# Splitting fp32 weights on GpSimd: gate/up part and down part with signals of their own

## The reference

```
x = x + tanh(g_xattn[0]) * attention(layernorm(x), ctx)          # 154 keys
x = x + tanh(g_ffn[0])   * sum over 8 experts e of
          (silu(xn @ Wg[e]) * (xn @ Wu[e])) @ Wd[e]              # 256 -> 1024 -> 256
x = x + tanh(g_xattn[1]) * multi_head_attention(layernorm(x), ctx)
x = x + tanh(g_ffn[1])   * top-1 mixture of 8 experts, 256 slots each
```

## Time and profile before

| | us |
|---|---|
| median of 3 runs | 1388.63 |
| lowest, highest | 1377.47, 1392.26 |
| the profiled execution | 1381.46 |
| its span, first to last instruction | 1379.6 |

### The profile page before, as it was taken

One profiled execution on the slowest core, in us unless ns is written; L12 is line 12 of the kernel. 1 busy time (PEld: TensorE's weight loads), 2 busy tenths in 40 slices (PEclk: granted clock), 3 DMA queues, 4 the chain that ended last, 5 costly groups with the idle time before them and its releaser, 6 DMA issues.

```text
span 1379.6 us, 18833 instructions
## 1 busy us (share of the span) xinstructions
PE 1268.5 (92%) x6162; PEld 1011.2 (73%) x6162; DVE 910.8 (66%) x1654; ACT 627.9 (46%) x1320; POOL 499.5 (36%) x501
## 2 busy tenths in 40 slices
PE   6979999999999999999999999999999999989945
PEld 4758777777777777777777777777777757767744
DVE  4886676666666666677666666666667647667533
ACT  2444444454444454444444445445444434443510
POOL 2342443333333344444333333344444003233324
PEclk9979999999999999999999999999999999999968
DMA  4040000100000000000100000000000321011033
GB/s 125 24 146 0 24 23 32 38 24 24 24 24 24 24 24 24 23 24 24 40 30 24 24 23 24 23 24 24 23 24 1 107 80 34 32 65 47 19 119 119
DMA packets 46646, 54.42 MB, mean 39 GB/s; under 512 B 4445, under 2 KB 42386, under 8 KB 46431
## 3 DMA queue, kind: packets, MB, share of 16 engines
q1 hardware_dynamic: 41360, 42.92, 9.6%
q0 software_dynamic: 3088, 9.76, 1.9%
q10 hardware_dynamic: 2111, 0.63, 0.2%
HBM read 37.35 MB, written 12.62 MB: 36 GB/s over the span
## 4 chain that ended last, share of the span: by engine, by line
PE 58%; POOL 29%; DVE 4%; issue 4%; ACT 2%; DMA 2%; DVEq 0%; POOLq 0%; ACTq 0%; SPq 0%
PE bank L896 16%; PE bank L897 15%; PE bank L898 15%; POOL w_lo L467 5%; POOL wd_lo L473 4%; POOL w_lo L469 3%; POOL w_raw L453 3%; POOL w_lo L471 2%; POOL w_hi L455 2%; POOL w_hi L465 2%; PE bank L1071 2%; POOL w_raw L452 2%; POOL w_raw L461 2%; POOL w_raw L457 2%; PE bank L1091 1%
## 5 line engine op out<-in xcount | busy, mean ns | idle before, releaser
L896 PE MATMUL bank<-xop_hi,w_hi 128*128 128x512 f32 x896 | 356.3, 398 | 48.0 <-POOL wd_lo L473 38.3
L897 PE MATMUL bank<-xop_lo,w_hi 128*128 128x512 f32 x896 | 353.3, 394 | 0.0
L898 PE MATMUL bank<-xop_hi,w_lo 128*128 128x512 f32 x896 | 352.2, 393 | 0.0
L1451 DVE TENSOR_TENSOR acc<-bank,acc 128x512 f32<-128x512 f32 x248 | 170.7, 688 | 186.1 <-PE bank L898 185.9
L896 PEld LDWEIGHTS bank<-xop_hi,w_hi 128*128 128x128 f32 x896 | 169.5, 189 | 100.6 <-issue 58.8
L452 POOL TENSOR_TENSOR w_raw<-raw_gu 128x256 f32<-128x256 f32 x32 | 23.7, 742 | 600.9 <-PE bank L898 600.9
L897 PE MATMUL bank<-hid_lo,wd_hi 128*128 128x512 f32 x512 | 203.0, 396 | 0.0
L896 PE MATMUL bank<-hid_hi,wd_hi 128*128 128x512 f32 x512 | 202.4, 395 | 0.7 <-DVE hid_lo L1437 0.7
L898 PE MATMUL bank<-hid_hi,wd_lo 128*128 128x512 f32 x512 | 201.3, 393 | 0.0
L898 PEld LDWEIGHTS bank<-xop_hi,w_lo 128*128 128x128 f32 x896 | 169.4, 189 | 38.2
L897 PEld LDWEIGHTS bank<-xop_lo,w_hi 128*128 128x128 f32 x896 | 169.7, 189 | 36.9
(11 more groups left out here) (188 smaller groups left out, 1701.4 us busy)
## 6 DMA issues: line engine op xcount, KB each, us to landing
raw_gu<-in_L_ffn_Wg_dram SPq DMA_DIRECT2D x32, 256.0 KB, 2.7
raw_gu<-in_L_ffn_Wu_dram SPq DMA_DIRECT2D x32, 256.0 KB, 3.1
raw_d<-in_L_ffn_Wd_dram SPq DMA_DIRECT2D x32, 256.0 KB, 3.7
slots<-empty_row POOLq DMA_DIRECT2D x1, 4112.0 KB
kept<-slots SPq DMA_DIRECT2D x8, 258.0 KB, 4.8
x_res<-in_x_dram SPq DMA_DIRECT2D x4, 512.0 KB, 5.3
we_raw<-in_L_ffn_W_dram SPq DMA_DIRECT2D x8, 256.0 KB, 4.3
out_dram<-x_res SPq DMA_DIRECT2D x4, 512.0 KB
```

The lines of the kernel that those rows point to most:

```text
L896: mm(ps, w, a, start=start, stop=False, skip_group_check=True)
L897: mm(ps, w, a_low, start=False, stop=False, skip_group_check=True)
L898: return mm(ps, w_low, a, start=False, stop=True, skip_group_check=True)
L1451: nc.vector.tensor_tensor(out=to, in0=ps, in1=to, op=ALU.add).then_inc(acc_added, 1)
```

## The change

`w_ready` becomes two signals, `gu_ready` and `wd_ready`, and in `split(q)` the two instructions of the down weights move from among the others to the end, behind a wait of their own. The wait ahead of the gate and up part is now for `p4_ps["u"]` (product4 of "u") of both groups of the quarter two before; the old wait on `down_ps` stands before the down part. TensorE waits for `gu_ready` where it waited for `w_ready`, and for `wd_ready` ahead of the first down product of a quarter. SyncE waits for `wd_ready`.

```diff
--- before.py
+++ after.py
@@ -295,7 +295,7 @@
         x_raw_ready, x_sum_ready, x_hi_ready, x_lo_ready = (
             sem(n) for n in ("x_raw_ready", "x_sum_ready", "x_hi_ready", "x_lo_ready"))
         raw_in = [sem(f"raw_in{i}") for i in range(2)]
-        w_steps, w_hi_ready, w_ready = (sem(n) for n in ("w_steps", "w_hi_ready", "w_ready"))
+        w_steps, w_hi_ready, gu_ready, wd_hi_ready, wd_ready = (sem(n) for n in ("w_steps", "w_hi_ready", "gu_ready", "wd_hi_ready", "wd_ready"))
         p1_ps, p2_ps, p3_ps, p4_ps, p5_ps, p6_ps, p7_ps = (
             {X: sem(f"p{i}_ps_{X}") for X in "gu"} for i in range(1, 8))
         forked, p5_kept, u2_kept, sum12, sum22 = (
@@ -337,7 +337,7 @@
             def load_weights(q):
                 e, f = q // (NQ // NE0), q % (NQ // NE0)
                 if q >= 2:
-                    sp.wait_ge(w_ready, q - 1)
+                    sp.wait_ge(wd_ready, q - 1)
                 cols, blocks = slice(f * FP, (f + 1) * FP), slice(2 * f, 2 * f + 2)
                 sp.dma_start(raw_gu[q % 2][:, 0], Wg_v[e, :, :, cols]).then_inc(raw_in[q % 2], 16)
                 sp.dma_start(raw_gu[q % 2][:, 1], Wu_v[e, :, :, cols]).then_inc(raw_in[q % 2], 16)
@@ -346,7 +346,7 @@
             for q in range(NQ):
                 load_weights(q)
 
-            sp.wait_ge(w_ready, NQ)
+            sp.wait_ge(wd_ready, NQ)
             sp.dma_start(Wkvs[:], Wkv.rearrange("(k p) n -> p k n", p=P)).then_inc(wc_in, 16)
             sp.dma_start(Wqs[:], Wq.rearrange("(k p) n -> p k n", p=P)).then_inc(wc_in, 16)
             sp.wait_ge(down_ps, 4 * (GROUPS - 2))
@@ -448,7 +448,7 @@
                 f0, f1 = slice(0, P), slice(P, 2 * P)
                 pool.wait_ge(raw_in[i], 48 * (q // 2 + 1))
                 if q >= 2:
-                    pool.wait_ge(down_ps, 4 * PAIRS * (q - 1))
+                    pool.wait_ge(p4_ps["u"], PAIRS * (q - 1))
                 nc.gpsimd.tensor_tensor(out=s[:, :, W_S1], in0=r[:, :, 0, f1], in1=r[:, :, 1, f1], op=ALU.add)
                 nc.gpsimd.tensor_tensor(out=s[:, :, W_S3], in0=r[:, :, 0, f0], in1=r[:, :, 0, f1],
                                         op=ALU.subtract).then_inc(w_steps, 1)
@@ -460,7 +460,6 @@
                 pool.wait_ge(w_steps, 3 * q + 2)
                 nc.gpsimd.tensor_tensor(out=s[:, :, W_S4], in0=r[:, :, 1, f0], in1=s[:, :, W_S2],
                                         op=ALU.subtract).then_inc(w_steps, 1)
-                nc.gpsimd.tensor_copy(wd_hi[i][:], d[:])
                 pool.wait_ge(w_steps, 3 * q + 3)
                 nc.gpsimd.tensor_copy(hi[:, :, W_S1:W_S4 + 1], s[:, :, W_S1:W_S4 + 1]).then_inc(w_hi_ready, 1)
                 pool.wait_ge(w_hi_ready, q + 1)
@@ -469,9 +468,13 @@
                 nc.gpsimd.tensor_tensor(out=lo[:, :, W_11:W_22], in0=r[:, :, :, f0],
                                         in1=hi[:, :, W_11:W_22].bitcast(F32), op=ALU.subtract)
                 nc.gpsimd.tensor_tensor(out=lo[:, :, W_22], in0=r[:, :, 1, f1], in1=hi[:, :, W_22].bitcast(F32),
-                                        op=ALU.subtract)
+                                        op=ALU.subtract).then_inc(gu_ready, 1)
+                if q >= 2:
+                    pool.wait_ge(down_ps, 4 * PAIRS * (q - 1))
+                nc.gpsimd.tensor_copy(wd_hi[i][:], d[:]).then_inc(wd_hi_ready, 1)
+                pool.wait_ge(wd_hi_ready, q + 1)
                 nc.gpsimd.tensor_tensor(out=wd_lo[i][:], in0=d[:], in1=wd_hi[i][:].bitcast(F32),
-                                        op=ALU.subtract).then_inc(w_ready, 1)
+                                        op=ALU.subtract).then_inc(wd_ready, 1)
 
             for u in range(NC):
                 power(u, CT, 1)
@@ -905,7 +908,7 @@
                     pe.wait_ge(x_hi_ready, 7 * p + X_ORDER.index(x) + 1)
                     pe.wait_ge(x_lo_ready, 7 * p + X_ORDER.index(x) + 1)
                 if p == 0:
-                    pe.wait_ge(w_ready, q + 1)
+                    pe.wait_ge(gu_ready, q + 1)
                 i = q % 2
                 return three(bank[ps[X]][:], w_hi[i][:, SIDE[X], w, :], w_lo[i][:, SIDE[X], w, :],
                              xop_hi[p][:, x, :], xop_lo[p][:, x, :], start)
@@ -962,6 +965,8 @@
                 turn, f = 4 * n + part // 2, part % 2
                 m = slice(turn % 2 * P, (turn % 2 + 1) * P)
                 i, j = n // PAIRS % 2, n % 2
+                if n % PAIRS == 0 and part == 0:
+                    pe.wait_ge(wd_ready, n // PAIRS + 1)
                 if turn == 0:
                     pe.wait_ge(x_raw_ready, KB * NC)
                 if f == 0 and turn >= 2:
@@ -973,7 +978,7 @@
                 if f == 1:
                     ins.then_inc(down_ps, 1)
 
-            pe.wait_ge(w_ready, 1)
+            pe.wait_ge(gu_ready, 1)
             pe.wait_ge(x_hi_ready, 2)
             for X in "gu":
                 mm(bank[FORK_BANK[X]][:], w_hi[0][:, SIDE[X], W_S1, :], xop_hi[0][:, X_T1, :], start=True, stop=True)
```

## The result

The changed kernel takes 1337.22 us (median of 4 runs, 1335.70 to 1338.12) against 1384.11 for the kernel before in the same comparison (1377.47 to 1392.26): a ratio of 0.9674, 95% interval 0.9629 to 0.9718. The profiled execution took 1335.70, its span 1333.9, against 1381.46 and 1379.6.

A forecast was written before the change was run, and what follows sets the result against it. TensorE was taken to be held up by 30 waits for GpSimd's weight split. 30 x 1.51 = 45.3 us off the profiled 1381.46 gives 1336.2, against the median 1343.3; 1338 us was chosen, range 1326 to 1352.

The forecast's parts named there:

- The wait goes, all of it: Gate and up part, released earlier, has about 20 us to spare; TensorE's wait for the split in 30 quarters disappears.
- 1.51 us per wait, not the 1.28 of the idle column: TensorE at quarter boundaries: the same VectorE instruction's spacing, 16.75 against 15.24 us, prices each wait; 30 give 45.3 us.
- The down part and the new wait cost nothing: Down part ends about 29 us before TensorE needs it; its new wait costs nothing, at most 3 us for 32.
- Loads and what lies behind the loop: nothing: Quarter loads go 10 us earlier with about 34 us of cover; next stage's weight load also goes earlier; no gain.
- GpSimd beside VectorE: nothing: The moved gate and up part meets VectorE's low parts of hidden blocks; a 0.98 us stretch stays hidden in 2.8 us.
- The first rival of the prediction: VectorE becomes late: low parts blocked by long GpSimd instructions make TensorE wait at its first down product; about 1366 us, chance 0.06.
- three times the stretch: Argument against VectorE becoming late: the low parts' slack, 2.8 us, against the 0.98 us stretch the trace shows.
- 1338 rather than 1336 or 1343: Choice between subtracting from the profiled execution (1336.2) and the median (1343.3), in case run spread leaves with the wait.
- The clock did not fall: Rival: TensorE's clock falls in the unbroken loop of about 975 us; at 0.93 it costs 73 us, about 1410; chance 0.03.
- The second rival: The wait at quarter boundaries was not the split's, so the gap would stay: 1381 to 1389 us, chance 0.04.

The follow-up runs named there:

- the two kernels with one half each: Against the kernel before: separate gate and up signal with the old release, 1327.4 us (0.9645); early release with TensorE waiting for the whole split, 1329.0 us (0.9665).
- the 512 waits: Changed kernel with the wait for the down part's signal ahead of each of 512 down products, not of 32: 1332.1 us, ratio 0.9658 to the kernel before.
- the kernel with the new order alone: Kernel before with only the split's two down instructions moved last, behind a wait; old release, TensorE waits for the whole split: 1382.8 us, ratio 1.0045.
- the two runs with padding on VectorE: Changed kernel plus three or six idle VectorE subtractions of 128x512 per iteration, ahead of a low part: 1337.7 us (0.9730) and 1645.2 us (1.1955).

## Why the prediction was right

1. *The wait goes, all of it.* Right. The gate and up part starts 0.40 us ahead of the even iteration, to the hundredth as worked out, and ends 10.6 us in, not 10.1, with the stretched instructions. The two kernels with one half each show that the lateness of 1.5 us is a threshold, not a sum, which the prediction had not said: I had costed the new release as the source of the gain, while moving two instructions behind a signal was enough.

2. *1.51 us per wait, not the 1.28 of the idle column.* Right. From the first copy into `acc` to the next stage's first matmul the loop took 1004.99 us before (103.51 to 1108.5) and takes 959.99 (101.41 to 1061.4): 45.0 less, where 45.3 was forecast and the idle column would have given 38.3. The rest of the 46.6 lies before that copy, 31.23 against 29.59, a stretch in which TensorE idles and runs partly at the low level in both kernels; the kernel with the new order alone, which keeps the 30 waits, has 29.45 there, so it isn't the removed wait's.

3. *The down part and the new wait cost nothing.* Right, and by the 512 waits the upper bound of 3 us was far too wide.

4. *Loads and what lies behind the loop: nothing.* In keeping with the trace: SyncE issues at 466.06, 6.1 us into the odd iteration, and no wait on a load appears. No run varied the loads by themselves.

5. *GpSimd beside VectorE: nothing.* Right in the result, too narrow in its bound. The pair of low parts grew by 0.63, within the 0.98 that I allowed. But the two runs with padding on VectorE show that such a pair grows by 2.45 and 3.22 when it falls beside GpSimd's instructions of 1024 columns. The first rival of the prediction named these and dismissed them, since the short ones stand there; that is so in this kernel. The claim that the slack is "three times the stretch" held only for this placement, and not at all in the loop's last iteration, where the low part is wanted 0.7 us in; there TensorE waits 0.7 us in both kernels, so the change lost nothing by it.

6. *1338 rather than 1336 or 1343.* The number came out 0.8 us from the median, and that is luck: the reason for it was wrong. I let part of the spread leave with the wait. The runs show that the spread stays, and in the changed kernel it is in the stages around the loop; where the kernel before has its spread is not shown, since only one execution of it was profiled. On another chip the same kernel took 1331.1, with the kernel before at 1381.6 beside it. The subtraction from the profiled execution, 1336.2, met the profiled 1335.7; the subtraction from the median then known, 1343.3, missed by 6.1, of which 4.5 are the median of three runs standing above that of four.

The clock did not fall: 1.00 over 960 us with 0.7 us of idle. The second rival, that the wait was not the split's, fell with the first trace.

## What to carry to other kernels

When an engine waits a little at a regular boundary, compare the work behind the wait with the time that it has, and look for what in that work the waiting engine doesn't need yet: a signal two instructions earlier was by itself worth 3.6% here (0.9645). Such a gain is a threshold: a second remedy adds no time, only margin, and margin is measured by padding. Price a wait by the distance between the same instruction in two rounds, not by the idle column.

## What the runs showed of the hardware

- 480 more waits that are already met, ahead of matmuls, changed a loop of 989.5 us by less than 0.4.
- TensorE's granted clock stayed at 2.4 GHz across idles of 1.28 us, 1.5 us (the kernel with the new order alone) and, once in a quarter, 2.17 us. After idles of 2.73, 3.02, 5.05 and 5.8 us the matmuls started 0.43 us apart, the 1.2 GHz level, for 2.7 to 6.1 us. But three matmuls behind an idle of 3.04 us were still at the full level, and those behind the 1.51 us that followed were not: the length of one idle doesn't decide alone, and what does is open.
- VectorE's subtractions of two SBUF operands, with GpSimd at work beside them, took 1.91, 3.73 and 4.50 us a pair, 1.28 alone; one of them took 2.82. In a row of eight beside the split each ended 0.53 to 0.55 us after a GpSimd instruction ended. GpSimd's own grew by 0.25 to 0.5 when they met.
